# Transposing layer-normed tiles without TensorE in two stages with low-rank experts

## The reference

```
x = x + 0.5 * ffn(layernorm(x))
x = x + attention(layernorm(x))        # 32 heads, 8 key heads, rotary, causal
x = x + 0.5 * ffn(layernorm(x))

def ffn(h):                            # 8 experts of rank 16, 2 chosen per row
    logits = h @ gate_w.T              # [rows, 8]
    w, chosen = top_k(logits, 2); w = softmax(w)
    w_full = scatter of w over the 8 experts
    low = h @ lora_A.T                 # [rows, 8 * 16]
    return h @ base_w.T + base_b + 2 * ((low * w_full) @ lora_B)
```

## Time and profile before

| what | value |
|---|---|
| median of 3 runs | 1513.42 us |
| profiled execution | 1512.09 us |
| its span, first to last instruction | 1510.3 us |
| mean granted TensorE clock | 0.999 of full |
| PE, PEld busy | 1483.6 us (98%), 1187.3 us (79%) |
| DVE, ACT, POOL busy | 953.0, 581.5, 697.3 us |
| bytes moved | 146.01 MB, mean 97 GB/s |

### The profile page before, as it was taken

The page is one execution under the profiler, slowest core; times in us unless marked ns, Lnnn a source line. Parts: engine busy times, 40 slices in busy tenths (PEclk is TensorE's granted clock), DMA queues, the critical chain, the costliest instruction groups (busy, mean ns, idle before and its releaser), DMA issues. The chain is left out here.

```text
span 1510.3 us, 25951 instructions
## 1 busy us (share of the span) xinstructions
PE 1483.6 (98%) x9216; PEld 1187.3 (79%) x9216; DVE 953.0 (63%) x2726; ACT 581.5 (39%) x1058; POOL 697.3 (46%) x384
## 2 busy tenths in 40 slices
PE   7999999999999999999999999999999999999999
PEld 7999999888888875555555555555489999999988
DVE  6645455655563858888998888888465343433433
ACT  4333332221211126666666666666542122221210
POOL 1332322443334438999999999999503010100100
PEclk9999999999999999999999999999999999999999
DMA  6323232542416162543333444330262112121201
GB/s 240 129 100 115 99 128 101 177 141 87 140 70 161 69 166 61 113 96 79 79 79 79 108 106 99 78 79 23 64 238 77 49 56 71 43 83 42 83 15 42
DMA packets 118725, 146.01 MB, mean 97 GB/s; under 512 B 40896, under 2 KB 77120, under 8 KB 118336
## 3 DMA queue, kind: packets, MB, share of 16 engines
q1 hardware_dynamic: 90304, 121.37, 28.0%
q10 hardware_dynamic: 28304, 23.14, 4.7%
HBM read 95.72 MB, written 53.51 MB: 99 GB/s over the span
## 5 line engine op out<-in xcount | busy, mean ns | idle before, releaser
L1698 ACT ACTIVATE at_probs<-ps 128x512 f32<-128x512 f32 (+1 forms) x640 | 314.9, 561 | 163.7 <-PE ps L1607 157.8
L69 DVE CUSTOM_DVE_ANT_0 ps<-ps,at_score_mask 128x512 f32<-128x512 f32 (+1 forms) x480 | 270.3, 622 | 23.5 <-PE ps L1596 21.8
L349 POOL TENSOR_TENSOR f_x_ring<-f_x_ring,f_half_bias 128x1024 f32<-128x1024 f32 x32 | 78.1, 2444 | 309.3 <-DVE f_h L638 303.1
L1539 POOL TENSOR_TENSOR at_added<-at_added,at_probs 128x2048 f32<-128x2048 f32 (+1 forms) x60 | 210.5, 3509 | 2.7 <-ACT at_probs L1698 0.9
L1624 PE MATMUL ps<-at_probs,at_vs 128*32 128x512 f32 (+3 forms) x1536 | 150.2, 494 | 0.3 <-POOL at_probs L1518 0.3
L75 PE MATMUL f_ps<-f_wt_hi,f_hT_hi 128*128 128x400 f32 (+1 forms) x384 | 133.4, 347 | 3.2 <-DVE f_hT_lo L642 3.2
L75 PE MATMUL ps<-f_wt_hi,f_hT_hi 128*128 128x400 f32 (+1 forms) x384 | 131.4, 342 | 0.0
L77 PE MATMUL f_ps<-f_wt_hi,f_hT_lo 128*128 128x400 f32 (+1 forms) x384 | 130.8, 341 | 0.0
L76 PE MATMUL f_ps<-f_wt_lo,f_hT_hi 128*128 128x400 f32 (+1 forms) x384 | 130.6, 340 | 0.0
L76 PE MATMUL ps<-f_wt_lo,f_hT_hi 128*128 128x400 f32 (+1 forms) x384 | 130.2, 339 | 0.0
L77 PE MATMUL ps<-f_wt_hi,f_hT_lo 128*128 128x400 f32 (+1 forms) x384 | 130.0, 338 | 0.0
(11 more groups left out here) (206 smaller groups left out, 3591.1 us busy)
## 6 DMA issues: line engine op xcount, KB each, us to landing
f_x_ring<-in_L_attn_resid SPq DMA_DIRECT2D x16, 512.0 KB, 3.5
x<-f_x_ring SPq DMA_DIRECT2D x16, 512.0 KB, 2.6
early<-x SPq DMA_DIRECT2D x16, 512.0 KB, 3.4
scr_q_hi<-qkv_rope_hi ACTq DMA_DIRECT2D x32, 256.0 KB, 2.0
scr_q_lo<-qkv_rope_lo ACTq DMA_DIRECT2D x32, 256.0 KB, 2.3
scr_ctx<-at_ctxn SPq DMA_DIRECT2D x32, 256.0 KB, 2.4
shared<-scr_ctx SPq DMA_DIRECT2D x16, 512.0 KB, 4.5
f_x_ring<-x SPq DMA_DIRECT2D x16, 512.0 KB, 3.7
```

What stands on the lines that cost most here:

```text
L69: return dve.tensor_tensor_reduce(out=src[:, 0:keys], in0=src[:, 0:keys], in1=mask, scale=1.0, scalar=part_max[:, g, own] if c else -3.0e3 ...
L349: pool.tensor_tensor(x_ring[:, u, :], x_ring[:, u, :], half_bias[:], ALU.add).then_inc(bias_added, 1)
L1539: pool.tensor_tensor(added[:, heads, :], first, probs[:, (NU * n + u) % PROBS, heads, :], ALU.add).then_inc(added_done, 1)
L1698: act.activation(probs[:, (NU * n + u) % PROBS, g, cols], score_ps[x % BANKS][:, cols], ACT.Exp, scale=SCALE).then_inc(exp_done, 1)
```

## The change

Tiles from `FROM` on (3 in the first stage, 1 in the second) are no longer turned by TensorE. VectorE writes `h` and then transposes it in squares of 32x32 into `blocks` (`to_blocks`), which leaves each square turned in its place. 16 transfers (`exchange`), one for each pair of a group of 32 rows and a group of 32 columns, move the squares between groups of partitions, from `blocks` into the slot of `hT_lo`. Each of them has 32 x 8 runs of 128 bytes. ScalarE then reads `hT_lo` instead of PSUM for `hT_hi`, and VectorE subtracts in place. `h_ready` of such a tile is counted by `to_blocks`, no more by `normalize`.

`blocks` is one buffer, so `to_blocks` of a tile waits until the exchange of the one before has landed. The exchange of tile t + 2 waits for part 0 of `lora(t)`, after which the slot of `hT_lo` is free. In the first stage it stands on SP ahead of the wait for `ffn_added` and the store of tile t; in the second behind the store. In the first stage the norm of tile t + 2 moves ahead of `low_lowT(t)` and `low_hT(t + 1)`, and `deviation` ahead of the wait for `ffn_done`. `high_hT` moves behind `high_lowT` in both. `turn_low` no longer waits for `low_hT` of the next tile.

```diff
+SQ = 32
+EXCHANGED = (P // SQ) ** 2 * 16
+def exchange(sp, blocks, landing, loaded):
+    for a in range(P // SQ):
+        for b in range(P // SQ):
+            src = blocks[a * SQ:(a + 1) * SQ, :].rearrange("i (c b j) -> i c b j", b=P // SQ, j=SQ)[:, :, b, :]
+            sp.dma_start(landing[b * SQ:(b + 1) * SQ, :, a * SQ:(a + 1) * SQ].bitcast(F32), src).then_inc(loaded, 16)
...
+    FROM = 3 if prep else 1
+        blocks = prep["early"][:, 3, :] if prep else sb("blocks", [P, D], F32)[:]
+        def landed(t):
+            return FROM + EXCHANGED * (t - FROM + 1)
...
+            def turn(t, par):
+                sp.wait_ge(h_ready, t + 1)
+                if not (isinstance(t, int) and t < 2):
+                    sp.wait_ge(ffn_done, 3 * t - 4)
+                exchange(sp, blocks, hT_lo[:, par, :, :], h_turned)
+            if attn:
+                turn(1, 1)
             def step(i, t, u, more):
...
+                    if u == 3:
+                        sp.wait_ge(h_turned, landed(NT - 1))
                     sp.dma_start(early[:, u, :], x_dst[u * P:(u + 1) * P, :]).then_inc(early_loaded, 16)
...
+                if prep and more >= 2 and not by_tensor(t + 2):
+                    turn(t + 2, u % 2)
                 sp.wait_ge(ffn_added, 3 * t + 6)
                 own = x_stored if prep and isinstance(t, int) and t == NT - 1 else stored[u]
                 sp.dma_start(x_dst[bass.ds(t * P, P), :], x_ring[:, u, :]).then_inc(own, 16)
+                if attn and more >= 2:
+                    turn(t + 2, u % 2)
...
             def turn_low(t, more):
                 pe.wait_ge(low_ready, t + 1)
+                pe.wait_ge(lowT_lo_done, t + 1)
...
             def lora(t, par):
                 pe.wait_ge(lowT_lo_done, t + 2)
+                if not (isinstance(t, int) and t < 2):
+                    pe.wait_ge(ffn_added, 3 * t + 3)
...
             def step(i, t, u, more):            # TensorE
-                if more >= 1:
-                    turn_h(t + 1)
                 base(t, u % 2, 0)
-                turn_low(t, more >= 1)
+                turn_low(t, False)
...
             def high_hT(t, par):
-                act.wait_ge(h_turned, t + 1)
-                act.activation(hT_hi[:, par, :, :], hT_ps, ACT.Copy).then_inc(hT_hi_done, 1)
+                if by_tensor(t):
+                    act.wait_ge(h_turned, t + 1)
+                else:
+                    act.wait_ge(h_turned, landed(t))
+                src = hT_ps if by_tensor(t) else hT_lo[:, par, :, :].bitcast(F32)
+                act.activation(hT_hi[:, par, :, :], src, ACT.Copy).then_inc(hT_hi_done, 1)
...
             def step(i, t, u, more):            # ScalarE
                 gap_exp(t)
+                if prep and more >= 2:
+                    deviation(t + 2)
                 act.wait_ge(ffn_done, 3 * t + 1)
+                high_lowT(t)
                 if more >= 1:
                     high_hT(t + 1, (u + 1) % 2)
-                high_lowT(t)
-                if more >= 2:
+                if attn and more >= 2:
                     deviation(t + 2)
...
+            def to_blocks(t):
+                if not by_tensor(t - 1):
+                    dve.wait_ge(h_turned, landed(t - 1))
+                wait_apart(dve, ln_step, norm_steps(t, 5), passed)
+                dve.transpose(blocks, h[:]).then_inc(h_ready, 1)
             def low_hT(t, par):
                 dve.wait_ge(hT_hi_done, t + 1)
-                dve.tensor_tensor(hT_lo[:, par, :, :], hT_ps, hT_hi[:, par, :, :].bitcast(F32),
+                src = hT_ps if by_tensor(t) else hT_lo[:, par, :, :].bitcast(F32)
+                dve.tensor_tensor(hT_lo[:, par, :, :], src, hT_hi[:, par, :, :].bitcast(F32),
...
                 layer_norm(0, 1, 1)             # start of the second stage
+                to_blocks(1)
                 for c in range(4, KC):
                     low_landed(c)
...
             def step(i, t, u, more):            # VectorE
                 routing(t, u % 2)
+                if prep and more >= 2:
+                    layer_norm(i, t + 2, u + 2)
+                low_lowT(t)
+                if prep and more >= 2:
+                    to_blocks(t + 2)
                 if more >= 1:
                     low_hT(t + 1, (u + 1) % 2)
-                low_lowT(t)
-                if more >= 2:
-                    if attn and not first_tile(t):
+                if attn and more >= 2:
+                    if not first_tile(t):
                         add_projection(i, t + 2, u + 2)
                     layer_norm(i, t + 2, u + 2)
                 if early_tile(t) is not None:
                     early_norm(u)
                 add_ffn(t, u)
+                if attn and more >= 2:
+                    to_blocks(t + 2)
```

More of the change, by code:

```diff
@@ L246, in first_tile, with by_tensor, norm_steps @@
             return isinstance(t, int) and t == 0
+        def by_tensor(t):
+            return isinstance(t, int) and t < FROM
+        def norm_steps(t, k):
+            return 4 * t + k + (0 if by_tensor(t) else t - FROM)
+        def landed(t):
+            return FROM + EXCHANGED * (t - FROM + 1)
         def load_x(eng, t, s):
@@ L500, in step @@
             def step(i, t, u, more):
-                if more >= 1:
-                    turn_h(t + 1)
+                if prep and isinstance(t, int) and t == 2:
+                    pe.wait_ge(ffn_added, 3 * t + 3)
                 base(t, u % 2, 0)
-                turn_low(t, more >= 1)
+                turn_low(t, False)
                 if attn and more >= 2 and not first_tile(t):
@@ L537, in high_hT @@
             def high_hT(t, par):
-                act.wait_ge(h_turned, t + 1)
-                act.activation(hT_hi[:, par, :, :], hT_ps, ACT.Copy).then_inc(hT_hi_done, 1)
+                if by_tensor(t):
[4 more added lines that the diff above has]
+                act.activation(hT_hi[:, par, :, :], src, ACT.Copy).then_inc(hT_hi_done, 1)
             def deviation(t):
-                act.wait_ge(ln_step, 4 * t + 3)
+                act.wait_ge(ln_step, norm_steps(t, 3))
                 act.activation(std[:], mv[:, 1:2], ACT.Sqrt, bias=eps[:, 0:1]).then_inc(std_ready, 1)
@@ L629, in moments @@
                     dve.bn_stats(stats[:, half, :], x[:, half * HALF:(half + 1) * HALF]).then_inc(ln_step, 1)
-                wait_apart(dve, ln_step, 4 * t + 2, passed)
+                wait_apart(dve, ln_step, norm_steps(t, 2), passed)
                 dve.bn_aggr(mv[:], stats[:, :, :].rearrange("p a b -> p (a b)")).then_inc(ln_step, 1)
@@ L635, in normalize @@
                 dve.reciprocal(rstd[:], std[:]).then_inc(ln_step, 1)
-                dve.wait_ge(ln_step, 4 * t + 4)
-                dve.wait_ge(h_turned, t)
-                dve.tensor_scalar(h[:], x_ring[:, u % 4, :], mv[:, 0:1], rstd[:, 0:1], ALU.subtract, ALU.mult).then_inc(h_ready, 1)
+                dve.wait_ge(ln_step, norm_steps(t, 4))
+                if by_tensor(t) or by_tensor(t - 1):
+                    dve.wait_ge(h_turned, t)
+                dve.tensor_scalar(h[:], x_ring[:, u % 4, :], mv[:, 0:1], rstd[:, 0:1], ALU.subtract, ALU.mult).then_inc(h_ready if by_tensor(t) else ln_step, 1)
+            def to_blocks(t):
[3 more added lines that the diff above has]
+                dve.transpose(blocks, h[:]).then_inc(h_ready, 1)
             def low_hT(t, par):
                 dve.wait_ge(hT_hi_done, t + 1)
-                dve.tensor_tensor(hT_lo[:, par, :, :], hT_ps, hT_hi[:, par, :, :].bitcast(F32),
+                src = hT_ps if by_tensor(t) else hT_lo[:, par, :, :].bitcast(F32)
+                dve.tensor_tensor(hT_lo[:, par, :, :], src, hT_hi[:, par, :, :].bitcast(F32),
                                   ALU.subtract).then_inc(hT_lo_done, 1)
@@ L750, in _ @@
                 add_ffn(1, 1)
+                to_blocks(3)
             else:
```

## The result

The changed kernel takes 1520.41 us (median of 20 runs, 1517.15 to 1525.09) where the kernel before takes 1514.51 (20 runs, 1510.16 to 1518.78): 1.0039 times as long, 95% interval 1.0029 to 1.005. It was forecast at 1493.5 and is slower. The profiled execution has a span of 1516.3 us, 6.0 more than before.

The account below looks back on a forecast made before the run. TensorE, busy 98% of the span, was taken to bound the kernel. Gains 9.6 + 0.7 + 12.2 - 2.5 = 20.0 us took 1512.1 to 1492.1, median 1.3 higher, said as 1493.5; range 1489 to 1499, chance 0.64.

Parts of the forecast that it names:

- The gap between issues: Exchange on SP: 16 issues per tile at 0.54 us each, 8.6 us, with ends of 0.38 and 0.63.
- The rest of SP's round: SP in the first stage, behind the issues: store, x load, Wq; 2.9 + 1.7 us per tile.
- SP's round does not fit: Rival, first stage: issues at 0.8 us make SP need 17.4 us a tile; about 1533 us; chance 0.10.
- The meeting: First stage: add_bias meets the next tile's routing; routing and low_hT end 1.05 us later, just hidden.
- Port lost twice: Rival, first stage: low_hT itself meets low_wq and add_bias, tile takes 16.4 us; about 1518 us; chance 0.10.
- The first stage: Tiles 4 to 15 gain 0.8 us each, 9.6 us; tile 3 adds 0.7.
- the slack: First-stage tile: low_hT ends at +8.2 us after MAX8, TensorE wants it at +10.0; 1.8 us spare.
- Tile 3: First exchanged tile of the first stage, without lead: net gain 0.7 us, bounds -1 and +1.6.
- The second stage's tiles: 14 second-stage tiles gain 0.87 us each, 12.2 us, with a period of about 25.2 us.
- Its start: Start of the second stage: late low_hT(1), adds and routing(1) cost 0.4 to 5 us, taken as 2.5.

Follow-up runs that it names:

- e5: Changed kernel, but each of the 16 transfers moves 1 KB in a row per partition instead of eight 128 B pieces (result not the reference): 1513.6 us.
- e2: Changed kernel, but each tile moved by 8 transfers of 64 partitions instead of 16 of 32, both stages (result not the reference): 1494.7 us.
- e6: Changed kernel, but blocks go through a DRAM scratch, 5 issues per tile instead of 16, with strided transpose writes and TensorE reads: 1650.8 us.
- e4: Changed kernel, but in the first stage GpSimd adds the half bias to only 8 columns of a tile: 1520.5 us.
- e9: Changed kernel, but in the first stage ScalarE issues six of a tile's 16 transfers, behind its high_hT, instead of SP: 1518.5 us.
- e13: e9 with GpSimd also adding the half bias to only 8 columns of a tile in the first stage: 1503.2 us.
- e12: e10, but ScalarE splits Wq before issuing its six transfers, and issues those of tile 3 behind gap_exp(2): 1494.5 us.
- e3: Changed kernel, but in the first stage SP issues the Wq load and weight copy ahead of its wait for the store: 1518.6 us.
- e10: e9, plus Wq and weight copy issued at the start of SP's step, and second-stage tile 1 turned by TensorE: 1513.5 us.
- e7: Changed kernel, but second-stage tile 1 is also turned by TensorE, so the new way begins at tile 2: 1516.3 us.
- e1: Changed kernel, but with the first stage as in the kernel before, so only the second stage is changed: 1511.8 us.

## Why the prediction was wrong, step by step

- **The gap between issues: the step that failed.** "I take 0.54, the nearest shape" should have read 0.65. The 0.54 row reads from DRAM, the 0.63 row goes from SBUF to SBUF as the exchange does. I chose by the pattern, and e5 and e2 show that it counts for little (0.63 with 32 pieces, 0.65 with 256, 0.67 with 512). e6's loads from DRAM into 32 partitions take a median of 0.43 us, e5's from SBUF, in runs of 1 KB too, 0.59. The 0.65 lies just outside even my ends of 0.38 and 0.63.
- **The rest of SP's round: mis-sized too.** I had 2.9 + 1.7 = 4.6 us behind the issues; it is 5.0 to 5.3. With 5.25 the round equals the old period of 15.14 at (15.14 - 5.25) / 16 = 0.62 us an issue, where my 4.6 gives 0.66. The 0.71 of the rival "SP's round does not fit" is another point, where the first stage's loss cancels a gain of 9.7 in the second; with 5.25, and the 6.3 that the second stage did gain, it moves to 0.65, the spacing that was measured. That rival had the mechanism, at a price of 0.8 that no issue of this kind has but the few long ones. These, one of 1.1 to 1.95 us in five of the exchanges, are in no term; they make up to 12.2 of 10.4.
- **The meeting.** Its place and price were right (L711 2.35 us, when Wq is late). That it costs nothing ("just hidden") hung on the 0.54; the sum that I gave for 0.63 has turn_low stall for 0.9 us, and the trace has 8.2 us in nine such waits. What I did not see is that a late SP makes both: TensorE waits for whichever is later, so neither edit alone pays (e4, e9), both together do (e13, e12, and e2 and e3, where one edit acts on both causes). "Port lost twice" has the time in its range (1510 to 1521), but by luck: low_hT takes 1.18 to 1.23 us, for 1.21 before, and was not what was blocked.
- **The first stage**, 9.6 + 0.7 us forecast, was -13.3. With half the issues it is +11.8, with two queues and Wq first +10.1. So transpose (1.25), landing (1.9), high_hT (1.06), low_hT (1.18) and the slack held; the period of 14.3 is real.
- **Tile 3** was to gain 0.7 us. It took 19.7 us for 16.9: its landing and low_hT were late, and TensorE's clock fell (below). With half the issues (e2) it takes 15.7 and in e12 15.6, gains of 1.2 and 1.3. Dividing the issues alone does not do it: in e9, e10 and e13, where `gap_exp` stands behind ScalarE's six, it takes 20.6 to 22.1.
- **The second stage's tiles** held to the figure of 25.2: 25.17 us from the fifth period on.
- **Its start** was put at 2.5 us and costs 4.0, inside the bounds of 0.4 to 5, which e7 gives back by leaving tile 1 to TensorE: 2.5 of lateness, with TensorE waiting for low_s as named, and 1.5 of clock, which is in no term. **Its last tile** I forgot: it has no projection to hide sixteen issues, TensorE waits 1.6 us for low_hT, and it takes 16.08 us, where e2 shows 14.26.

The terms add up: 23.6 us missed in the first stage, 3.4 in the second (9.7 forecast, 6.3 measured), -1.0 elsewhere, together the 26 us between -20.0 and +6.0 in the span.

## What to carry to other kernels

Price a queue of small transfers by its issues: take the gap from a row with the same source and destination memory, add what else that engine issues in the round, and compare the sum with the period before asking when the data lands. Where one late engine feeds two consumers, expect two bounds, and don't take an experiment that removes one of them without gain as proof that it is harmless. The remedy was to divide the issues between two engines and to put the short steps, whose results others need, ahead of the long run of issues.

## What the runs showed of the hardware

The 0.65 us of an issue belongs to the issuing engine: in e9 ScalarE and SP issued side by side at 0.65 and 0.73 us, where taking turns would have put 1.3 between the issues of each. The Trainium skill's page "DMA: Bandwidth & Descriptors" (Issuing engines are not separate DMA queues) says that a second issuing engine saves no more than the time to initiate, usually small beside the transfer; here it was 10.4 of the 15.7 us of SP's round, and not small.

TensorE's clock can fall after a pause. In the changed kernel TensorE was all but idle from 226 to 229 us. The windows of that pause, behind it, and behind the wait of 2.5 us for low_s at the start of the second stage:

```profile
226.00:229.00 3.00, 0.26 (x2) 0.00 (x0) 2.45 (x6) 1.45 (x3) 0.46 (x1) 1.00 0.63 120
229.00:233.00 4.00, 3.29 (x10) 3.27 (x11) 3.68 (x11) 1.25 (x3) 3.33 (x2) 0.62 0.33 54
...
1162.00:1165.00 3.00, 3.00 (x9) 2.32 (x8) 0.29 (x1) 0.18 (x1) 0.00 (x0) 0.50 0.24 38
```

A granted clock of 0.50 is 1.2 GHz, and only nine matmuls begin in 3 us. Both kernels have such a stretch in the first 20 us and one at the very end; the changed kernel has three more, of 3.4 us each (from 62.7, 229.9 and 1161.8 us). Each costs about half of that, an estimated 1.7 us, on top of the pause: that is part of tiles 3 and 14 and of the second stage's start. In the tile windows shown first, with pauses of 1.3 to 1.5 us in all, it stayed at 1.00.

A pause does not always bring it. The second stage of e9 begins with the same wait, and its clock stays at 1.00; it is that stage which is 1.5 us shorter:

```profile
PE ps L480 <- DVE f_low_s L732: 2.5, 1, 2.5
...
1152.00:1165.00 13.00, 10.11 (x53) 9.03 (x52) 7.92 (x19) 1.14 (x3) 7.78 (x3) 1.00 0.27 68
```

And in e1 it fell between the stages where TensorE had waited no longer than 0.9 us. What decides it is not shown here. The medians show its weight: the granted clock is 0.994 in the runs of the changed kernel and 0.996 to 0.997 in those of the kernel before beside the experiments. That is an estimated 3 to 4.5 of the 5.9 us by which the changed kernel is slower; a pause on TensorE has to be counted with it.
